# Query weight restacked in the first batch, and each later key matrix from 16 matmuls of 128 rows and 16 of 64

## Chip, cores and metric

The kernel runs on one core of one Trainium2 chip. The time is the device time of one execution in microseconds; lower is better.

## The reference

Eight sequences (batches) of 1024 rows and 1024 columns pass through cross-attention with a context of 64 rows each, and then through a linear layer in simulated fp8, both with a residual:

```
x = x + xattn(layernorm(x), ctx, Wq, Wkv, Wout)
    qp = q @ Wq.T ;  k, v = split(ctx @ Wkv.T)          # 16 heads of 64
    scores = (qh . kh) / 8, causal mask over 1024 x 64
    attn = softmax(scores) ;  out = (attn @ vh) @ Wout.T
x = x + ffn(layernorm(x), weight)
    both operands quantised to e4m3 by their largest magnitude,
    out = (x8 @ w8.T) * scales, rounded to bf16
```

## The kernel before

*What it computes with.* Sequences are cut into tiles of 128 rows: TB = 8 tiles in a batch, B = 8 batches, T = 64 tiles. Queries are never formed. For each batch a key matrix M = Wq' K' is made, 1024 columns (16 heads of 64 keys) by 1024 input columns, in CT = 8 pieces of 128 input columns; scores of a tile are then x times M (`scores`, matmuls in L730). In the same way N holds the values times Wout, and the output of a tile is p times N (`split_product`, L746). Numbers are carried as a high and a low half in f16, and a product is three matmuls: high by high, high by low, low by high (`PASSES`, L349). A tile takes 48 matmuls in L730 and 48 in L746.

*How a key matrix is made before.* `make_m(ct, n)` (L675) makes piece ct. For each of the NP = 8 pairs of heads j it goes through the three passes, and in each pass issues two matmuls (L683): the even head on partitions 0 to 63 (`EVEN`) and the odd head on 64 to 127 (`ODD`). Each has 64 rows of contraction, 128 columns of weights and 64 columns moved, so a piece is 48 matmuls. The weights come from `wq_nat[s]` (s = 0 high, 1 low half of Wq; rows of head pair j on the partitions) and the moving side from `k_rows[:, s, j]`, or for batch 0 from `k_split` (`first_m`, which calls `make_m`). The even heads' results go to one PSUM bank, the odd heads' to another (`place`). Pieces alternate between the PSUM regions ps_p and ps_x; a region is free again when ScalarE has taken the high half (L994) and VectorE the low half (L1271) of the piece before it: `grow_full`, `grow_hi`, `grow_free`.

*Where it stands in the order.* The pieces for batch b+1 are made in the seventh tile step (tt = TB - 2 = 6) of batch b, two at a time: pieces 0 and 1 inside the scores of tile t+1 behind chunk 6 (`KEYS_AT_S`), and pieces 2 and 3, 4 and 5, 6 and 7 inside the output product of tile t (`KEYS_AT_O`). The pieces for N are made in a like way with matmuls of 64 rows by 64 columns (L713). That makes 28 such places in the kernel for batches 1 to 7; batch 0's are made before the first tile.

*SP's queue* issues all DMAs in a fixed order: in each step the store of the finished tile (L478), at tt = 0 (for batch 0 at tt = 3) the keys of the next batch from DRAM (`next_k`, `load_k`, L421), at tt = 5 the values, then the load of x four tiles ahead (L403), the DMA transpose of x two tiles ahead (`turn_x`, L429), the second load of x for the residual (L403) and the transpose of p (`turn_p`, L432). In batch 0 the FFN weight (`load_w8`, L471) is loaded in two halves behind steps 2 and 4, to `w8_raw`, which until then holds `k_split`. VectorE first reads it in steps 2 to 5 of batch 1 (`AMAX_AT`).

The stages of a tile on VectorE and ScalarE (layer norm, softmax, splits into halves, residual) run one or two tiles ahead of, or behind, TensorE's. After the last tile the FFN phase runs (L903), from about 1485 us.

Of the kernel before, what the change touches and what calls it, by code (L numbers as in the profile page):

```python
# [25 lines left out]
F16 = mybir.dt.float16  # L26
# [7 lines left out]
P = 128  # L34
# [22 lines left out]
def xattn_ffn_kernel(nc, x, ctx, Wq, Wkv, Wout, Wffn, out):  # L57
# [3 lines left out]
    NP = NH // 2  # L61
# [13 lines left out]
    with ExitStack() as scope:  # L75
# [12 lines left out]
        wo_t = sb("wo_t", [P, 2, NP, H], F16)  # L88
        m_buf = sb("m_buf", [P, 2, CT, H], F16)
        n_buf = sb("n_buf", [P, 2, NP, H], F16)  # L90
        k_rows = sb("k_rows", [P, 2, NP, SK], F16)
        v_rows = sb("v_rows", [P, 2, NP, SK], F16)

        w8_raw = sb("w8_raw", [P, CT, H], BF16)
# [73 lines left out]
        wkv_t = wo_t[:, 1].rearrange("p j c -> p (j c)").bitcast(F32).rearrange("p (a q) -> p a q", a=LT)  # L168
        w8_flat = w8_raw[:].rearrange("p j c -> p (j c)").bitcast(F16)
        k_split = [w8_flat[:, i:i + 4096].rearrange("p (j k) -> p j k", k=KEYS) for i in (0, 4096)]  # L170
        V_SLOTS = (9, 10, 11, 2)
        v_split = [tile_space[:, i, :].bitcast(F16).rearrange("p (s j k) -> p s j k", s=2, k=KEYS) for i in V_SLOTS]
        wq_nat = [wq_stack[:].rearrange("p (j e) c -> p e j c", e=2)[:, s] for s in (0, 1)]
# [31 lines left out]
        kv_stored = sem("kv_stored")  # L205
        got_k = sem("got_k")
        got_v = sem("got_v")
        got_xa = [sem("got_xa0"), sem("got_xa1")]
        got_xr = [sem("got_xr0"), sem("got_xr1")]
        var_ready = sem("var_ready")  # L210
# [182 lines left out]
        def _(sp):  # L393
# [23 lines left out]

            def load_k(of):

                for s in range(2):  # L420
                    sp.dma_start(k_rows[:, s], of(s)).then_inc(got_k, 16)  # L421

            def load_v(of):
                for s in range(2):
# [49 lines left out]
            def step(b, tt, e, t):  # L474
                known = isinstance(t, int)
                if not (known and (t == 0 or t > KEPT)):
                    sp.wait_ge(x1_ready, t + 1)
                    sp.dma_start(x1_dram[bass.ds((t - 1) * P, P), :], x1[1 - e]).then_inc(x1_stored[1 - e], 16)  # L478
                if is_step(tt, 3 if b == 0 else 0) and not (known and t >= T - TB):
                    next_k(b + 1)  # L480
                if is_step(tt, 5) and not (known and t >= T - TB):
                    next_v(b + 1)
                if not known or t + 2 < T:
                    sp.wait_ge(x_lo, t + 3)
                    if not known or t + 4 < T:
                        load_x(xa, got_xa, t + 4, e)
                    turn_x(t + 2, e)
                if not known or t + 1 < T:
                    sp.wait_ge(p_lo, t + 2)
                    load_x(xr, got_xr, t + 1, 1 - e)  # L490
                    if not (known and t + 2 == T):
                        turn_p(t + 1, 1 - e)
                if b == 0 and tt in (2, 4):
                    sp.wait_ge(k_stored, 32)
                    load_w8(tt // 2 - 1)

            for b in range(B):
                batch(sp, b, step, unroll=b in (0, B - 1))
# [99 lines left out]
        def _(pe):  # L598
# [73 lines left out]
            expand(7)  # L672


            def make_m(ct, n, keys=lambda s, j: k_rows[:, s, j, :]):  # L675
                to = grow_ps[ct % 2]
                if not is_step(n, 0):
                    pe.wait_ge(grow_free[ct % 2], n)
                for j in range(NP):
                    for i, (ws, ks) in enumerate(PASSES):  # L680
                        for k, rows in enumerate((EVEN, ODD)):
                            h = 2 * j + k
                            mm = nc.tensor.matmul(to[:, place(h) * SK:(place(h) + 1) * SK],  # L683
                                                  wq_nat[ws][rows, j, ct * P:(ct + 1) * P], keys(ks, j)[rows],
                                                  start=(i == 0), stop=(i == len(PASSES) - 1))
                mm.then_inc(grow_full[ct % 2], 1)

            def first_m(ct):
                make_m(ct, ct // 2, lambda s, j: k_split[s][:, j, 0:SK])


            WOUT_FREE = ((kv_read, 7), (grow_free[0], 4), (grow_free[1], 4), (wout_lo, 1), (wout_lo, 2),
# [79 lines left out]
            def step(b, tt, e, t):  # L772
# [5 lines left out]
                if not known or t + 1 < T:  # L778
# [2 lines left out]
                    pe.wait_ge(x_turned, 16 * t + 32)  # L781
                    pe.wait_ge(s_read, t + 1)
                    if m_next:
                        pe.wait_ge(got_k, 32 * b + 32)
                        if b == 2:
                            pe.wait_ge(w_scale_made, 1)
                        if b >= 3:
# [928 lines left out]
```

## Time and profile before

| | us |
|---|---|
| median of 3 runs | 1732.33 |
| lowest and highest | 1732.08, 1732.6 |
| the profiled execution's own time | 1734.19 |
| its span, first to last instruction | 1732.3 |
| TensorE busy with matmuls, share of the span | 98% |
| TensorE weight loads, share | 47% |
| VectorE busy, share | 77% |
| ScalarE busy, share | 39% |

Engines are PE (TensorE's matmuls), PEld (TensorE's weight loads, which overlap PE), DVE (VectorE), ACT (ScalarE), POOL (GpSimd) and SPq (the queue on which SyncE issues DMAs). A matmul's end is modelled: its record is longer than the time until the next one starts, so the distance from start to start is what it takes in a dense stream. In a timeline a row is a run of like instructions, with its start, its length to the end of the last one, and how many there are.

### The profile page before, as it was taken

The page shows a single profiled execution, that of the slowest core. Times are in us where ns is not written, and L with a number is a line of the kernel's source. Part 1 is how long each engine was busy: PE and PEld are TensorE (multiplying, and loading weights), DVE is VectorE, ACT ScalarE, POOL GpSimd, SP SyncE. Part 2 cuts the span into 40 slices and gives each one's busy share as a digit, 9 for nine tenths or more (in the row PEclk, how much of TensorE's full clock was granted, in tenths as well). Part 3 has the DMA queues.
Part 4 walks back from the last instruction along what each step waited for, and adds up shares of the span by engine and source line. Part 5 has one row for each costly group of instructions (what it writes and reads, how often), then busy time and mean ns, then how long its engine had stood idle before and what let it go on. Part 6 is the DMA issues. An engine that isn't in the chain of part 4 may idle for free.

```text
span 1732.3 us, 27825 instructions
## 1 busy us (share of the span) xinstructions
PE 1705.6 (98%) x11485; PEld 809.8 (47%) x11513; DVE 1336.9 (77%) x1910; ACT 671.8 (39%) x638; POOL 182.7 (11%) x142
## 2 busy tenths in 40 slices
PE   7999999999999999999999999999999999999998
PEld 4544444445444544454445444544454444544444
DVE  7977687788866887788778877787779666877786
ACT  5632243223322332233223322332233222799985
POOL 0000000000000000000000000000000002255565
PEclk9999999999999999999999999999999999999999
DMA  9346645553545555545454445544544443799997
GB/s 351 105 106 168 152 90 126 135 143 93 128 121 131 111 124 114 140 108 128 121 128 123 119 126 130 113 106 126 132 124 110 97 86 74 263 310 331 320 251 216
DMA packets 387977, 258.95 MB, mean 149 GB/s; under 512 B 341920, under 2 KB 344480, under 8 KB 387616
## 3 DMA queue, kind: packets, MB, share of 16 engines
q1 hardware_dynamic: 387872, 257.47, 56.3%
q8 instruction: 76, 1.25, 0.3%
q14 instruction: 29, 0.24, 0.0%
HBM read 113.25 MB, written 67.11 MB: 104 GB/s over the span
## 4 chain that ended last, share of the span: by engine, by line
PE 86%; DVE 10%; ACT 2%; DMA 1%; issue 1%; SPq 0%; DVEq 0%; ACTq 0%
PE ps_all L730 36%; PE ps_all L746 33%; PE ps_all L903 12%; DVE m_buf L1271 3%; PE ps_all L713 3%; PE ps_all L683 1%; PE ps_all L755 1%; DVE tile_space L1340 1%; DVE hsum L1334 1%; DVE tile_space L1282 1%; DVE tile_space L1328 1%; PE ps_all L832 1%; DVE hmax L1323 1%; ACT tile_space L1007 1%; ACT tile_space L1011 1%
## 5 line engine op out<-in xcount | busy, mean ns | idle before, releaser
L730 PE MATMUL ps_all<-m_buf,tile_space 128*128 128x504 f16 x3072 | 667.7, 376 | 0.6 <-DVE m_buf L1271 0.3
L746 PE MATMUL ps_all<-n_buf,tile_space 128*128 128x512 f16 x3024 | 667.4, 379 | 0.5 <-DMA tile_space<-tile_space 0.5
L730 PEld LDWEIGHTS ps_all<-m_buf,tile_space 128*128 128x128 f16 x3072 | 297.8, 98 | 351.8 <-issue 6.7
L746 PEld LDWEIGHTS ps_all<-n_buf,tile_space 128*128 128x128 f16 x3024 | 293.1, 98 | 356.5 <-issue 7.0
L575 POOL TENSOR_TENSOR rstd_x<-veps_x,minus_half 128x1 f32<-128x1 f32 x64 | 35.3, 551 | 1397.1 <-DVE veps_x L1295 1397.1
L1015 ACT ACTIVATE tile_space<-tile_space,neg_mean 128x1024 f32<-128x1024 f32 x56 | 64.4, 1149 | 279.6 <-DVE neg_mean L1360 279.6
L1011 ACT ACTIVATE tile_space<-tile_space,score_scale 128x1024 f32<-128x1024 f32 x64 | 73.4, 1147 | 232.3 <-DVE tile_space L1328 232.3
L1007 ACT ACTIVATE tile_space<-tile_space 128x1024 f16<-128x1024 f32 x64 | 67.6, 1056 | 190.3 <-DVE tile_space L1340 190.3
L1282 DVE SCALAR_TENSOR_TENSOR tile_space<-tile_space 128x1024 f16<-128x1024 f32 x64 | 78.4, 1225 | 70.7 <-ACT tile_space L1007 70.7
L1334 DVE TENSOR_REDUCE hsum<-tile_space 128x16 f32<-128x1024 f32 x64 | 77.9, 1217 | 58.3 <-ACT tile_space L1011 58.3
L1277 DVE SCALAR_TENSOR_TENSOR tile_space<-tile_space 128x1024 f16<-128x1024 f32 x64 | 78.3, 1223 | 52.8 <-ACT tile_space L1001 52.8
L903 PE MATMUL ps_all<-wo_t,wq_stack 128*128 128x512 bf16 x482 | 114.0, 379 | 0.7
L1001 ACT ACTIVATE tile_space<-tile_space 128x1024 f16<-128x1024 f32 x64 | 67.6, 1056 | 113.5 <-DVE tile_space L1300 113.5
L1323 DVE TENSOR_REDUCE hmax<-ps_all 128x16 f32<-128x1008 f32 x64 | 77.1, 1204 | 30.8 <-PE ps_all L730 30.5
L989 ACT ACTIVATE n_buf<-ps_all 128x1024 f16<-128x1024 f32 x64 | 62.7, 1020 | 85.6 <-PE ps_all L713 85.6
L1632 DVE SCALAR_TENSOR_TENSOR n_buf<-ps_all,n_buf 128x1024 f32<-128x1024 f32 x64 | 78.2, 1221 | 22.4 <-ACT n_buf L1161 20.9
L1271 DVE SCALAR_TENSOR_TENSOR m_buf<-ps_all,m_buf 128x1008 f16<-128x1008 f32 x64 | 75.1, 1202 | 24.2 <-ACT m_buf L994 24.2
L1348 DVE SCALAR_TENSOR_TENSOR tile_space<-ps_all,out_scale,tile_space 128x1024 f32<-128x1024 f32 x56 | 71.7, 1280 | 27.0 <-PE ps_all L746 27.0
L903 PE MATMUL ps_all<-wo_t,tile_space 128*128 128x512 bf16 x389 | 89.8, 379 | 1.2 <-ACT tile_space L1168 0.4
L1265 DVE SCALAR_TENSOR_TENSOR n_buf<-ps_all,n_buf 128x1024 f16<-128x1024 f32 x64 | 75.9, 1219 | 13.5 <-ACT n_buf L989 13.5
L1168 ACT ACTIVATE tile_space<-ps_all,small 128x1024 bf16<-128x1024 f32 x63 | 70.2, 1114 | 30.8 <-PE ps_all L903 28.8
L1289 DVE BATCH_NORM_STATS2 stats_a<-tile_space 128x6 f32<-128x512 f32 x128 | 81.7, 680 | 0.0
(170 smaller groups left out, 1565.9 us busy)
## 6 DMA issues: line engine op xcount, KB each, us to landing
tile_space<-in_x_dram SPq DMA_DIRECT2D x128, 512.0 KB, 4.0
x_scratch<-tile_space SPq DMA_DIRECT2D x56, 512.0 KB, 3.1
m_buf<-x_scratch SPq DMA_DIRECT2D x32, 512.0 KB, 5.6
out_dram<-m_buf SPq DMA_DIRECT2D x32, 512.0 KB, 4.3
tile_space<-x_scratch SPq DMA_DIRECT2D x24, 512.0 KB, 6.0
out_dram<-tile_space SPq DMA_DIRECT2D x24, 512.0 KB, 5.1
m_buf<-in_L_xattn_Wq_dram SPq DMA_DIRECT2D x4, 1024.0 KB, 12.0
n_buf<-in_L_xattn_Wout_dram SPq DMA_DIRECT2D x4, 1024.0 KB, 13.1
```

The source lines that it names most:

```text
L730: mm = nc.tensor.matmul(ps_s[:, half * HALF:half * HALF + RH], left[:, ls, c * P:(c + 1) * P], m_buf[:, rs, c, half * RH:(half + 1) * RH], ...
L746: mm = nc.tensor.matmul(to[:, cols], left[:, ls, j * P:(j + 1) * P], right[:, rs, j, cols], start=(c == 0 and i == 0), stop=(c == CT - 1 a ...
L903: mm = nc.tensor.matmul(y_ps[e][:, cols], left[:, c * P:(c + 1) * P], w8_t[:, c, cols], start=(c == 0), stop=(c == CT - 1))
L1007: nc.scalar.activation(p_rows2[:, 0, :], pr, ACT.Copy, scale=P_SCALE).then_inc(p_hi, 1)
L1011: nc.scalar.activation(ex, sub, ACT.Exp, scale=score_scale[:]).then_inc(exp_done, 1)
L1271: nc.vector.scalar_tensor_tensor(out=keys_of(1, c), in0=rest_of(grow_ps[c % 2][:]), scalar=M_SCALE, in1=keys_of(0, c), op0=ALU.mult, op1=A ...
L1277: nc.vector.scalar_tensor_tensor(out=x_rows2[:, 1, :], in0=xn[e], scalar=XN_SCALE, in1=x_rows2[:, 0, :], op0=ALU.mult, op1=ALU.subtract).t ...
L1282: nc.vector.scalar_tensor_tensor(out=p_rows2[:, 1, :], in0=pr, scalar=P_SCALE, in1=p_rows2[:, 0, :], op0=ALU.mult, op1=ALU.subtract).then_ ...
L1289: nc.vector.bn_stats(stats_a[:, half, :], xa[e][:, half * HALF:(half + 1) * HALF]).then_inc(a_stats, 1)
L1323: nc.vector.tensor_reduce(by_bank(hmax[:]), rest_scores, AX.X, ALU.max).then_inc(max_done, 1)
L1334: nc.vector.tensor_reduce(hsum[:], heads(ex), AX.X, ALU.add).then_inc(sum_done, 1)
L1632: nc.vector.scalar_tensor_tensor(out=a_t[e], in0=u_ps[e], scalar=ROUND_LEAST, in1=v_t[e], op0=ALU.max, op1=ALU.add).then_inc(a_done, 1)
```

## The change

The low half of the query weight and the keys are laid out anew. In steps 1 to 3 of batch 0 five DMAs within SBUF swap halves of `wq_nat`, so that `wq_nat[0]` then holds, for each even head, the high half on partitions 0 to 63 and the low half on 64 to 127, and `wq_nat[1]` for each odd head the low half on 0 to 63 and the high half on 64 to 127. `low_moved`, over the memory of `w8_raw`, is the place between. `load_k` loads the high half of the keys twice, on both halves of the partitions: `k_rows[:, 0]` for even heads, `k_rows[:, 1]` for odd heads, and the low half to `k_rows[:, 2]`. So one matmul of 128 rows gives high by high plus low by high for a head. `make_m` then issues for each pair j two matmuls of 128 rows (one a head) and two of 64 rows (high weight by low key): 32 for a piece, with accumulation groups now of two matmuls a head. The first batch's pieces are made as before by `first_m`, which has the old loop. The FFN weight's halves are loaded behind steps 6 and 7 of batch 0, and TensorE waits once for the restacked weight.

```diff
-        k_rows = sb("k_rows", [P, 2, NP, SK], F16)
+        k_rows = sb("k_rows", [P, 3, NP, SK], F16)
+        low_moved = w8_flat.rearrange("p (j c) -> p j c", c=H)
+        w_moved = sem("w_moved")
             def load_k(of):
-                for s in range(2):
-                    sp.dma_start(k_rows[:, s], of(s)).then_inc(got_k, 16)
+                for k, head in enumerate((EVEN, ODD)):
+                    for rows in (EVEN, ODD):
+                        sp.dma_start(k_rows[rows, k], of(0)[head]).then_inc(got_k, 16)
+                sp.dma_start(k_rows[:, 2], of(1)).then_inc(got_k, 16)
+
+            def stack_wq(tt):
+                if tt == 1:
+                    sp.wait_ge(k_stored, 32)
+                    for k in range(2):
+                        sp.wait_ge(grow_full[k], 4)
+                    for to, of in ((ODD, EVEN), (EVEN, ODD)):
+                        sp.dma_start(low_moved[to], wq_nat[1][of]).then_inc(w_moved, 16)
+                if tt == 2:
+                    sp.wait_ge(w_moved, 32)
+                    sp.dma_start(wq_nat[1][ODD], wq_nat[0][ODD]).then_inc(w_moved, 16)
+                if tt == 3:
+                    sp.wait_ge(w_moved, 48)
+                    for k, rows in enumerate((ODD, EVEN)):
+                        sp.dma_start(wq_nat[k][rows], low_moved[rows]).then_inc(w_moved, 16)
...
-                if b == 0 and tt in (2, 4):
-                    sp.wait_ge(k_stored, 32)
-                    load_w8(tt // 2 - 1)
+                if b == 0 and tt in (1, 2, 3):
+                    stack_wq(tt)
+                if b == 0 and tt in (6, 7):
+                    sp.wait_ge(w_moved, 80)
+                    load_w8(tt - 6)
...
-            def make_m(ct, n, keys=lambda s, j: k_rows[:, s, j, :]):
+            def make_m(ct, n):
                 to = grow_ps[ct % 2]
-                if not is_step(n, 0):
+                pe.wait_ge(grow_free[ct % 2], n)
+                head = lambda h: to[:, place(h) * SK:(place(h) + 1) * SK]
+                for j in range(NP):
+                    for k in range(2):
+                        nc.tensor.matmul(head(2 * j + k), wq_nat[k][:, j, ct * P:(ct + 1) * P], k_rows[:, k, j, :],
+                                         start=True, stop=False)
+                    for k, rows in enumerate((EVEN, ODD)):
+                        mm = nc.tensor.matmul(head(2 * j + k), wq_nat[k][rows, j, ct * P:(ct + 1) * P],
+                                              k_rows[rows, 2, j, :], start=False, stop=True)
+                mm.then_inc(grow_full[ct % 2], 1)
+
+            def first_m(ct):
+                n = ct // 2
+                to = grow_ps[ct % 2]
+                if n > 0:
                     pe.wait_ge(grow_free[ct % 2], n)
...
                     if m_next:
-                        pe.wait_ge(got_k, 32 * b + 32)
+                        pe.wait_ge(got_k, 80 * b + 80)
+                        if b == 0:
+                            pe.wait_ge(w_moved, 80)
```

## Rows read from the trace of the kernel before

**Rows 1.** The page: busy time by engine, granted clock in 40 slices, chain, two groups.

```profile
PE 1705.6 (98%) x11485; PEld 809.8 (47%) x11513; DVE 1336.9 (77%) x1910; ACT 671.8 (39%) x638; POOL 182.7 (11%) x142
PEclk9999999999999999999999999999999999999999
PE 86%; DVE 10%; ACT 2%; DMA 1%; issue 1%; SPq 0%; DVEq 0%; ACTq 0%
L730 PE MATMUL ps_all<-m_buf,tile_space 128*128 128x504 f16 x3072 | 667.7, 376 | 0.6 <-DVE m_buf L1271 0.3
L746 PE MATMUL ps_all<-n_buf,tile_space 128*128 128x512 f16 x3024 | 667.4, 379 | 0.5 <-DMA tile_space<-tile_space 0.5
```

**Rows 2.** Waits, 104 to 1467 us, TensorE: in total, times, longest, in us.

```profile
PEld ps_all L713 <- issue: 11.8, 28, 0.4
PEld ps_all L683 <- issue: 8.9, 21, 0.4
PEld ps_all L683 <- DVE m_buf L1271: 4.4, 14, 0.4
PE ps_all L746 <- DMA tile_space<-tile_space: 0.5, 1, 0.5
```

**Rows 3.** Busy time in a stretch: bounds, length, PE, PEld, DVE, ACT, POOL, clock, DMA.

```profile
205.00:245.00 40.00, 39.91 (x541) 20.81 (x540) 30.60 (x47) 14.16 (x15) 1.10 (x2) 1.00 0.47 107
```

**Rows 4.** Timeline of TensorE, parts of batch 0: start, length in us, instructions.

```profile
146.16 10.36 PE L730 MATMUL ps_all<-m_buf,tile_space 128*128 128x504 f16 x48
...
187.28 2.93 PE L730 MATMUL ps_all<-m_buf,tile_space 128*128 128x504 f16 x13
...
197.48 10.52 PE L746 MATMUL ps_all<-n_buf,tile_space 128*128 128x512 f16 x48
207.84 7.81 PE L730 MATMUL ps_all<-m_buf,tile_space 128*128 128x504 f16 x36
215.59 1.57 PE L683 MATMUL ps_all<-k_rows,wq_stack 64*128 64x64 f16 x96
217.09 2.72 PE L730 MATMUL ps_all<-m_buf,tile_space 128*128 128x504 f16 x12
...
233.34 1.83 PE L683 MATMUL ps_all<-k_rows,wq_stack 64*128 64x64 f16 x96
235.10 1.24 PE L730 MATMUL ps_all<-m_buf,tile_space 128*128 128x504 f16 x5
```

**Rows 5.** The key matmuls' line in batches 1 to 7: durations in ns, forms.

```profile
L683 PEld LDWEIGHTS ps_all<-k_rows,wq_stack x2688: 92/95/97, 215.6 to 1298.8; 64*128 64x128 f16 x192
L683 PE MATMUL ps_all<-k_rows,wq_stack x2688: 189/190/201, 215.6 to 1298.9; 64*128 64x64 f16 x192
```

**Rows 6.** Timeline of TensorE in short windows at the first block's edges.

```profile
215.28 0.38 PE L730 MATMUL ps_all<-m_buf,tile_space 128*128 128x504 f16 x1
215.59 0.20 PE L683 MATMUL ps_all<-k_rows,wq_stack 64*128 64x64 f16 x2
...
216.91 0.25 PE L683 MATMUL ps_all<-k_rows,wq_stack 64*128 64x64 f16 x6
217.09 0.60 PE L730 MATMUL ps_all<-m_buf,tile_space 128*128 128x504 f16 x2
```

**Rows 7.** The same where a block of L713 ends, batch 0.

```profile
98.59 0.63 PE L713 MATMUL ps_all<-wo_t,v_rows 64*64 64x512 f16 x8
99.15 0.39 PE L746 MATMUL ps_all<-n_buf,tile_space 128*128 128x512 f16 x1
```

**Rows 8.** Full-height matmuls of 128 columns: timeline, and their line's durations in ns.

```profile
1469.94 0.61 PE L755 MATMUL ps_all<-ident_half,tile_space 128*128 128x128 f16 x8
...
L755 PE MATMUL ps_all<-ident_half,tile_space x16: 216/219/220, 1468.2 to 1470.3; 128*128 128x128 f16 x16
```

**Rows 9.** Timeline of SP's queue in batch 0 and at batch 1's first step.

```profile
125.90 3.31 SPq L432 DMA_TRANSPOSE tile_space<-tile_space  x1
...
135.19 3.51 SPq L429 DMA_TRANSPOSE tile_space<-tile_space  x1
...
148.91 0.58 SPq L471 DMA_DIRECT2D w_raw<-in_L_ffn_weight_dram  x1
...
150.08 3.55 SPq L421 DMA_DIRECT2D k_rows<-kv_scratch  x2
155.38 1.40 SPq L403 DMA_DIRECT2D tile_space<-in_x_dram  x1
...
165.99 3.59 SPq L432 DMA_TRANSPOSE tile_space<-tile_space  x1
...
176.31 3.29 SPq L429 DMA_TRANSPOSE tile_space<-tile_space  x1
...
262.67 1.90 SPq L421 DMA_DIRECT2D k_rows<-kv_scratch  x2
271.30 0.35 SPq L403 DMA_DIRECT2D tile_space<-in_x_dram  x1
```

**Rows 10.** DMA issues of the kernel: count, KB each, median us to landing.

```profile
kv_scratch<-w_raw SPq DMA_DIRECT2D x2, 1024.0 KB, 8.0
...
w_raw<-in_L_ffn_weight_dram SPq DMA_DIRECT2D x2, 1024.0 KB, 6.6
...
tile_space<-tile_space SPq DMA_TRANSPOSE x127, 5.5
...
v_rows<-tile_space SPq DMA_DIRECT2D x8, 32.0 KB, 2.2
```

**Rows 11.** Busy time around the clock's fall and in the FFN phase's start.

```profile
26.00:28.00 2.00, 0.30 (x1) 0.14 (x1) 1.93 (x5) 1.80 (x4) 0.00 (x0) 1.00 1.02 406
28.00:32.00 4.00, 3.96 (x18) 3.63 (x19) 3.48 (x9) 2.17 (x4) 0.00 (x0) 0.57 1.03 410
...
1498.00:1502.00 4.00, 2.37 (x17) 1.05 (x15) 3.79 (x5) 3.65 (x4) 0.20 (x1) 1.00 0.34 66
```

More of the change, by code:

```diff
@@ L683, in make_m @@
                             mm = nc.tensor.matmul(to[:, place(h) * SK:(place(h) + 1) * SK],
-                                                  wq_nat[ws][rows, j, ct * P:(ct + 1) * P], keys(ks, j)[rows],
+                                                  wq_nat[ws][rows, j, ct * P:(ct + 1) * P], k_split[ks][rows, j, 0:SK],
                                                   start=(i == 0), stop=(i == len(PASSES) - 1))
                 mm.then_inc(grow_full[ct % 2], 1)
-            def first_m(ct):
-                make_m(ct, ct // 2, lambda s, j: k_split[s][:, j, 0:SK])
             WOUT_FREE = ((kv_read, 7), (grow_free[0], 4), (grow_free[1], 4), (wout_lo, 1), (wout_lo, 2),
```

## Prediction, made before the changed kernel was run

> **What bounds the kernel now.** I read the page first, then the totals of waits on the middle of the run, then TensorE's timeline of one batch's seventh tile step (tt = 6), and last short windows at the edges of one block of key matmuls. The page gives TensorE 98% of the span at a granted clock of nine tenths or more in every slice, and the chain that ended last lies 86% on TensorE, 36% in L730 (scores) and 33% in L746 (output product) [rows 1]. The waits say the same more sharply: from 104 us to 1467 us TensorE's matmuls wait for another engine or a DMA once, 0.5 us at L746 [rows 2]. VectorE is busy 30.60 of 40 us around the step that the change touches [rows 3]. So in this stretch every nanosecond that the change adds to TensorE's own stream is a nanosecond of the span, and the question is only how long the new stream takes.
>
> **The stream as it is.** In the step that starts at 207.84 us there are four blocks of 96 key matmuls, each block two key matrices of 48 [rows 4]. Seven batches have them: 28 blocks, 2688 matmuls [rows 5]. A dense L730 stream has 48 matmuls in 10.36 us of which the last one's modelled 0.376 us is its tail: 9.98 / 47 = 0.212 us from start to start [rows 4, 1]. The block's edges differ from that [rows 6]:
> - Going in: the last L730 starts at 215.28 and the first key matmul at 215.59, 0.31 us later where 0.212 is usual: 0.096 us more.
> - Inside: the two matmuls of a pair (even and odd head, upper and lower 64 rows) start within 0.01 us of each other, both done 0.20 us after the first began, at 0.19 us each. The last pair starts at 217.16 - 0.19 = 216.97; from 215.59 that is 47 steps in 1.38 us, 0.029 us for a pair, so two matmuls of 64 rows run side by side in the time of one. 64 columns at 2.4 GHz are 0.027 us.
> - Going out: the first full-height L730 starts at 217.09, 0.12 us after the last pair, where 0.029 would follow: 0.092 us more. The L730 after it starts at 217.69 - 0.376 = 217.31, 0.22 us on, about 0.01 above the usual.
>
> The same is seen where L713 (64 rows by 64 columns) ends: the last of eight starts at 99.22 - 0.38 = 98.84, L746 at 99.15, 0.31 against 0.216 [rows 7]. It is no semaphore: no wait is charged at these edges, only "issue", in 28 of 28 entries of L713 and in 21 of L683 [rows 2]; and L730 runs on from L746 through its own waits with no added gap, 197.48 to 207.84 in 48 steps of 0.216 [rows 4]. What the edges share is that the row height changes between 128 and 64. Price of one change of height: 0.092 to 0.096 us.
>
> **The change, part by part.** (1) *Count of matmuls.* Before, a head pair j takes 3 pairs, 3 x 0.029 = 0.088 us. After, it takes 2 full-height matmuls, one after the other, and 1 pair: again 3 time slots, if a full-height matmul of 64 columns takes a slot of 0.029 us. The trace has no such matmul. Its bounds: 0.029 from below (64 columns stream in 0.027), and from above 0.056, the spacing of full-height loads with 128 columns: 8 in 0.61 us, (0.61 - 0.219) / 7 [rows 8]. I take the lower one, since the pairs load two 64 x 128 weights in every 0.029. So 48 matmuls become 32 and nothing is saved: the removed ones ran beside others.
>
> (2) *Order.* In the new loop j runs full, full, pair, and then full again. A key matrix changes height 16 times, where before a block of two changed it twice. Working for one j: full to full 0.029 + 0.01 (the second matmul after a change, as going out) = 0.039; full to pair 0.029 + 0.096 = 0.125; within the pair 0.003; pair to the next full 0.122. Sum 0.289 us. A block has 16 of these, 4.62 us; before it took 217.09 - 215.28 - 0.21 = 1.60 us. That is 3.02 us more in each block, 28 x 3.02 = 84.6 us. Nothing covers it, because TensorE waits for nobody there.
>
> (3) *What is given back.* The fourth block takes 1.76 us instead of 1.50 (233.34 to 235.10 against 215.59 to 217.09): its second matrix waits for VectorE's L1271, 14 times in the kernel with 4.4 us, and two of those waits belong to a batch [rows 4, 2]. With each matrix three times as long, VectorE, which has 1.21 us for a matrix, is done before. That returns 7 x 0.26 = 1.8 us. Behind the later blocks x, p and the residual come later by as much as TensorE does, so no other wait turns up; VectorE and ScalarE only get slack.
>
> (4) *The first batch.* Restacking adds five SBUF to SBUF transfers of 1 MB on SP's queue: two behind the transpose that ends its issue at 129.21, one in the place of the weight load at 148.91, two after 169.58 [rows 9]. SP itself is held for 0.6 us for each, as by that load. They go ahead of the transposes issued at 135.19 and 176.31 (L429), whose product TensorE takes up at 146.16 and 187.28; a transpose lands 5.5 us after issue, leaving 5.5 us of slack at both [rows 4, 9, 10]. A 1 MB move takes 6.6 us (HBM to SBUF) or 8.0 (SBUF to HBM) from issue to landing [rows 10]; a 32 KB move takes 2.2. If the second's 2.2 us overlap the first's data, two take 6.6 + 4.4 = 11.0 us, else up to 16, so from 129.8 they last until between 141 and 146. Behind 141 the transposed x is in by 145, in time; behind 146 it is in at 149, 3 us late, and that twice. Bounds 0 and +6 us; I take 0, because the step of 148.91 already has such a 1 MB and the keys ahead of its transpose with no wait at L730. The waits that SP gains there (stored keys, all first matrices full, the previous move) are met by then, or hold only what is queued behind them: the next x1 store and transposes. The FFN weight comes at steps 6 and 7 instead of 2 and 4; nobody reads it before step 2 of batch 1.
>
> (5) *Keys of a batch.* load_k has 5 transfers of 3072 pieces instead of 2 of 2048. The two hold SP for 3.55 us, or 1.90 later; times 1.5 that is at most 1.8 us more. In batch 0 the next x load waits from 153.63 to 155.38, in batch 1 from 264.57 to 271.30: covered but for 0.1 us, and that inside the 5.5 us above [rows 9]. The keys themselves are used a whole batch later. Cost 0.
>
> Sum: 84.6 - 1.8 = +82.8 us. The profiled execution took 1734.19 us with a span of 1732.3; what lies around the span (1.9 us) does not change, so it would go to 1817.0. The median of the runs shown, 1732.33, is 1.86 lower, and by the same sum it goes to **1815.1 us**.
>
> One rule of the Trainium skill goes beyond the rows here. TensorEngine Tiling (Array Packing), section Key Properties, says that switching the tiling mode, as against the tile, drains the engine. The trace agrees at each block edge (0.092 to 0.096 us), but it shows no switch between two matmuls of 64 columns; by the rule the 840 new switches cost the same there (+82.8), and without it the sum would be about -3.
>
> **Rivals.**
> - *The clock falls.* In the new blocks TensorE streams 24 slots of 0.027 us in 2.31, less than three tenths of the time. The trace has one fall inside the kernel, to 1.2 GHz: after a stretch in which the engine was busy 0.30 of 2.00 us, the mean granted clock from 28 to 32 us is 0.57, which is 3.44 us at half, 1.72 us lost [rows 11]. Against: it stayed at full through 1498 to 1502 with TensorE busy 2.37 of 4.00 us, and the new gaps are 0.1 us each [rows 11]. After every block that is 28 x 1.72 = 48 us, 1863; after half of them 1839.
> - *No drain between short matmuls.* Then a block is 48 slots, 48 x 0.0294 = 1.41, no cost at entry, 0.09 at exit: 1.50 against 1.60. 28 x -0.10 = -2.7 us, **1729.6 us**, the other side (not slower). For it: the height changes are only seen beside 504 and 512 columns on one side. Against: the exit follows a 64-column pair and pays in full. It decides below 7 ns a switch: 840 x 7 = 5.9 us would eat the 2.7 and 0.2% more.
> - *Only one direction costs* inside the loop, say the pair's loads go ahead while the full matmul of the other bank runs: 448 x 0.096 = 43 less, 1772. Against: both directions cost at the edges.
> - *A full-height load is not hidden.* If the second full matmul waits for its load, whose record is 0.095 us long [rows 5], it starts 0.10 after the first instead of 0.039: 448 x 0.06 = 27 more, 1842. Against it: the 0.056 of rows 8. The skill's page TensorE: Matmul & The Clock Gate, section LDWEIGHTS (loading the stationary operand), gives columns / 1.2 ns whatever the rows, 107 ns here, about 1846 us by that estimate; the trace disagrees, it fits such loads in 56 ns.
>
> **How the numbers follow.** Forecast 80%, clock 8%, no drain 5%, one direction 4%, load 3%. The range around the forecast: below, a full slot without the 0.01 (-4.5), a change of height 3 ns cheaper over 896 of them (-2.7) and 2 us for rows read to 10 ns, 1806; above, the full slot at 0.056 (+7.6), 3 ns more (+2.7), transfers (+6), the 1.8 not given back, 1833. The other cases lie outside, 20% together. A measurement of this kernel tells 0.2% (3.5 us) from no change: slower 94%, the same 4% and faster 2%, both from the case without a drain.
>
> **What would show it.** TensorE's timeline: blocks of 64 matmuls, about 4.6 us long, the step at 207.84 about 39 us instead of 27.3; matmuls of the key line at starts 0.04, 0.12, 0.00, 0.12 us apart. "Issue" waits of its loads in hundreds. No wait for a DMA at 146 and 187 us. A granted clock below full in the middle slices, blocks under 2 us, or a first batch longer than 207.84 us at the same place would each make this prediction wrong in its own term.

## The result, and the profile of the changed kernel

The changed kernel takes 1872.26 us (median of 4, 1872.01 to 1875.05) against 1732.3 before: 1.081 times as long, 95% interval 1.0795 to 1.0821, 140 us more. The forecast was slower, by 83 us, with a range that ended at 1833.

The page of the changed kernel first: busy time, granted clock in 40 slices, and the two lines that now make the key matrices (L702 the matmuls of 128 rows, L705 those of 64). Columns as in [rows 1].

```profile
span 1870.0 us, 26089 instructions
PE 1839.8 (98%) x10617; PEld 875.2 (47%) x10617; DVE 1341.7 (72%) x1910; ACT 676.2 (36%) x638; POOL 182.8 (10%) x142
PEclk9999989998999899999999999989998999999999
L702 PE MATMUL ps_all<-k_rows,wq_stack 128*128 128x64 f16 x896 | 106.2, 202 | 0.0
L705 PE MATMUL ps_all<-k_rows,wq_stack 64*128 64x64 f16 x896 | 92.6, 203 | 0.0
```

TensorE still has 98% of the span, with 868 matmuls fewer than before in the records (10617 against 11485; the program issues 896 fewer). New is the line of the clock: five slices of 40 are below nine tenths, where all were full in [rows 1]. Mean granted clock of the span is 0.973, before 0.999.

The timeline of TensorE in short windows at the start of the first block, which answers to [rows 6]:

```profile
222.13 0.38 PE L762 MATMUL ps_all<-m_buf,tile_space 128*128 128x504 f16 x1
222.34 0.22 PE L702 MATMUL ps_all<-k_rows,wq_stack 128*128 128x64 f16 x2
222.49 0.20 PE L705 MATMUL ps_all<-k_rows,wq_stack 64*128 64x64 f16 x2
222.63 0.23 PE L702 MATMUL ps_all<-k_rows,wq_stack 128*128 128x64 f16 x2
222.79 0.20 PE L705 MATMUL ps_all<-k_rows,wq_stack 64*128 64x64 f16 x2
...
226.83 0.23 PE L702 MATMUL ps_all<-k_rows,wq_stack 128*128 128x64 f16 x2
226.99 0.20 PE L705 MATMUL ps_all<-k_rows,wq_stack 64*128 64x64 f16 x2
227.13 4.41 PE L762 MATMUL ps_all<-m_buf,tile_space 128*128 128x504 f16 x12
```

Read the starts. Scores to the first full-height matmul: 0.21, no extra, for no height changes there. From then on a head pair starts every 0.30 us (222.49 to 222.79), where three slots of 0.029 would be 0.09. Finer: full to full 0.04, full to pair 0.125, within the pair 0.004, pair to full 0.131. The block fills 222.34 to 227.13, 4.79 us, where [rows 6] had 215.49 to 217.09, 1.60, counted from the usual 0.21 us behind the last score matmul. The last row has a second thing to see: 12 score matmuls take 4.41 us, which in [rows 4] took 2.72.

Busy time and granted clock in four stretches, columns as in [rows 3]: the block itself, a part of the 12 score matmuls behind it, the second block, and the whole run between launch phase and FFN phase.

```profile
222.34:227.13 4.79, 4.79 (x66) 3.35 (x64) 1.25 (x2) 1.96 (x2) 0.00 (x0) 1.00 0.00 0
227.72:231.13 3.41, 3.41 (x10) 1.21 (x8) 1.71 (x2) 0.53 (x1) 0.00 (x0) 0.50 0.54 153
233.97:238.96 4.99, 4.99 (x65) 3.40 (x64) 2.70 (x3) 2.16 (x2) 0.00 (x0) 0.90 0.00 0
...
104.00:1605.00 1501.00, 1493.83 (x8413) 701.02 (x8412) 1057.00 (x1591) 398.55 (x378) 42.87 (x62) 0.97 0.47 113
```

In the first block the clock is full. Just behind it, it is at 0.50, 1.2 GHz, for 3.41 us of dense scores. The second block ends with the clock already down: it takes 4.99 us at a mean of 0.90. The engine's modelled busy share in the block is 4.79 of 4.79, and it hides that the array streams columns for only 24 slots of 0.027 us in each half of the block.

The third difference is in the first batch. TensorE's waits from 104 to 1605 us, then SP's queue and TensorE's timeline there, and DMA issues with KB and median us to landing:

```profile
PE ps_all L762 <- DMA tile_space<-tile_space: 6.6, 2, 4.0
```

```profile
127.54 1.32 SPq L433 DMA_DIRECT2D w_raw<-wq_stack  x2
...
133.66 10.50 SPq L448 DMA_TRANSPOSE tile_space<-tile_space  x1
...
149.96 7.90 SPq L424 DMA_DIRECT2D k_rows<-kv_scratch  x4
...
170.54 1.31 SPq L440 DMA_DIRECT2D wq_stack<-w_raw  x2
...
177.25 13.10 SPq L448 DMA_TRANSPOSE tile_space<-tile_space  x1
```

```profile
147.11 10.37 PE L762 MATMUL ps_all<-m_buf,tile_space 128*128 128x504 f16 x48 [2.56 <-DMA tile_space<-tile_space]
...
192.43 12.06 PE L762 MATMUL ps_all<-m_buf,tile_space 128*128 128x504 f16 x48 [4.04 <-DMA tile_space<-tile_space]
```

```profile
w_raw<-wq_stack SPq DMA_DIRECT2D x2, 1024.0 KB, 9.6
wq_stack<-w_raw SPq DMA_DIRECT2D x2, 1024.0 KB, 12.0
```

The transposes of x behind each pair of restacking transfers hold SP 10.50 and 13.10 us at issue, where they held it 3.51 and 3.29 in [rows 9], and TensorE's scores wait 2.56 and 4.04 us for them. The 12.06 us of the second scores, against 10.36, are again the clock, after that wait.

Three sources stand side by side: longer blocks, a lower clock, waits of the first batch. The experiments take them apart. Times are medians, each compared with the kernel before on the same chip (1732.6 to 1733.0 us).

### The profile page after: what moved, and what is told of

Read it like the earlier page. It is cut to its first block, busy times and chain, and to the rows that moved or that the text cites. A ratio compares the mean times of both kernels' runs of the same rounds, so it can differ in the third digit from the quotient of the medians.

```text
span 1870.0 us, 26089 instructions
## 1 busy us (share of the span) xinstructions
PE 1839.8 (98%) x10617; PEld 875.2 (47%) x10617; DVE 1341.7 (72%) x1910; ACT 676.2 (36%) x638; POOL 182.8 (10%) x142
## 4 chain that ended last, share of the span: by engine, by line
PE 91%; DVE 5%; DMA 2%; ACT 1%; issue 0%; SPq 0%; DVEq 0%; ACTq 0%
PE ps_all L762 34%; PE ps_all L778 34%; PE ps_all L937 12%; PE ps_all L702 4%; PE ps_all L705 3%; PE ps_all L745 2%; DMA tile_space<-tile_space 2%; PE ps_all L787 1%; PE ps_all L866 1%; DVE wq_stack L1273 0%; DVE small L1267 0%; DVE wo_t L1292 0%; DVE n_buf L1299 0%; DMA tile_space<-_L_xattn_Wkv_expand_dram 0%; DVE tile_space L1279 0%
## 5 line engine op out<-in xcount | busy, mean ns | idle before, releaser
L762 PE MATMUL ps_all<-m_buf,tile_space 128*128 128x504 f16 x3072 | 690.9, 385 | 7.2 <-DMA tile_space<-tile_space 6.6
L778 PE MATMUL ps_all<-n_buf,tile_space 128*128 128x512 f16 x3024 | 685.2, 386 | 0.6 <-DMA tile_space<-tile_space 0.6
L762 PEld LDWEIGHTS ps_all<-m_buf,tile_space 128*128 128x128 f16 x3072 | 303.3, 100 | 376.4 <-issue 40.2
L778 PEld LDWEIGHTS ps_all<-n_buf,tile_space 128*128 128x128 f16 x3024 | 297.3, 99 | 370.4 <-issue 31.0
L1028 ACT ACTIVATE m_buf<-ps_all 128x1008 f16<-128x1008 f32 x64 | 64.6, 1011 | 149.2 <-PE ps_all L705 144.2
L702 PE MATMUL ps_all<-k_rows,wq_stack 128*128 128x64 f16 x896 | 106.2, 202 | 0.0
L705 PE MATMUL ps_all<-k_rows,wq_stack 64*128 64x64 f16 x896 | 92.6, 203 | 0.0
```

What stands on the lines that cost most here:

```text
L702: nc.tensor.matmul(head(2 * j + k), wq_nat[k][:, j, ct * P:(ct + 1) * P], k_rows[:, k, j, :], start=True, stop=False)
L705: mm = nc.tensor.matmul(head(2 * j + k), wq_nat[k][rows, j, ct * P:(ct + 1) * P], k_rows[rows, 2, j, :], start=False, stop=True)
L762: mm = nc.tensor.matmul(ps_s[:, half * HALF:half * HALF + RH], left[:, ls, c * P:(c + 1) * P], m_buf[:, rs, c, half * RH:(half + 1) * RH], ...
L778: mm = nc.tensor.matmul(to[:, cols], left[:, ls, j * P:(j + 1) * P], right[:, rs, j, cols], start=(c == 0 and i == 0), stop=(c == CT - 1 a ...
```

## Experiments

### Is it the change of height? Grouping the matmuls

> The changed kernel, but each key matrix issues its 16 matmuls of 128 rows first and then its 16 of 64 rows, so a block of two matrices changes the row height 4 times instead of 32. Same matmuls, same DMAs. Theory (the change of height costs about 0.13 us of drain each and the long stretch of drains makes the clock fall): a block goes from 4.79 us back to 48 slots x 0.029 + 4 x 0.1 = 1.8 us, no clock falls in the key steps, and what is left is +6 us for the blocks and +8.6 us for the restacking transfers: 1747 us. Rival (a matmul of 128 rows and 64 columns is dear in itself, or the low activity of short matmuls lets the clock fall): the block stays above 3 us and the time above 1800 us.

```diff
-                for j in range(NP):
-                    for k in range(2):
-                        nc.tensor.matmul(head(2 * j + k), wq_nat[k][:, j, ct * P:(ct + 1) * P], k_rows[:, k, j, :],
-                                         start=True, stop=False)
-                    for k, rows in enumerate((EVEN, ODD)):
-                        mm = nc.tensor.matmul(head(2 * j + k), wq_nat[k][rows, j, ct * P:(ct + 1) * P],
-                                              k_rows[rows, 2, j, :], start=False, stop=True)
+                for j0 in range(0, NP, 8):
+                    for j in range(j0, j0 + 8):
+                        for k in range(2):
+                            nc.tensor.matmul(head(2 * j + k), wq_nat[k][:, j, ct * P:(ct + 1) * P], k_rows[:, k, j, :],
+                                             start=(j == 0), stop=False)
+                    for j in range(j0, j0 + 8):
+                        for k, rows in enumerate((EVEN, ODD)):
+                            mm = nc.tensor.matmul(head(2 * j + k), wq_nat[k][rows, j, ct * P:(ct + 1) * P],
+                                                  k_rows[rows, 2, j, :], start=False, stop=(j == NP - 1))
```

Measured: 1744.05 us, ratio 1.007 (1.0053 to 1.0086). TensorE's timeline at the first block:

```profile
219.73 0.63 PE L703 MATMUL ps_all<-k_rows,wq_stack 128*128 128x64 f16 x16
220.29 0.41 PE L707 MATMUL ps_all<-k_rows,wq_stack 64*128 64x64 f16 x16
220.63 0.64 PE L703 MATMUL ps_all<-k_rows,wq_stack 128*128 128x64 f16 x16
221.21 0.41 PE L707 MATMUL ps_all<-k_rows,wq_stack 64*128 64x64 f16 x16
221.55 2.30 PE L764 MATMUL ps_all<-m_buf,tile_space 128*128 128x504 f16 x10
```

The same 64 matmuls now take 1.82 us (219.73 to 221.55) instead of 4.79, with only their order changed. Sixteen full-height ones take 219.73 to 220.29 with the way out, 0.56 us: 15 x 0.029 + 0.125. The clock is full in every block (mean of the span 1.000). The total is 3 us under the expected 1747. That fells the first half of the rival: a matmul of 128 rows and 64 columns is not dear, its slot is 0.029 us.

> The changed kernel, but the product with the low keys is also made with matmuls of 128 rows (the low keys loaded on both halves of the partitions too, 8 key transfers of 64 rows; the product low by low comes in addition): 32 matmuls of 128 rows and 64 columns for a matrix, in the interleaved order of the changed kernel, and no change of row height at all. Theory (only the change of height drains): a block is 64 slots of 0.029 = 1.87 us, no clock falls, 28 x 0.27 = +7.5 us, transfers +8.5, the wait of the fourth block gone -1.8: 1747 us. Rival (the gaps come from switching between PSUM banks or from going back to an open accumulation group, which this order keeps): blocks of 3 to 5 us, over 1790 us.

```diff
-        k_rows = sb("k_rows", [P, 3, NP, SK], F16)
+        k_rows = sb("k_rows", [P, 4, NP, SK], F16)
...
+                for j in range(NP):
+                    for s in range(2):
+                        for k in range(2):
+                            mm = nc.tensor.matmul(head(2 * j + k), wq_nat[k][:, j, ct * P:(ct + 1) * P],
+                                                  k_rows[:, 2 * s + k, j, :], start=s == 0, stop=s == 1)
```

Measured: 1745.12 us, 1.0075 (1.0059 to 1.009). The block:

```profile
219.67 2.03 PE L703 MATMUL ps_all<-k_rows,wq_stack 128*128 128x64 f16 x64
221.53 2.71 PE L760 MATMUL ps_all<-m_buf,tile_space 128*128 128x504 f16 x12
```

64 slots in 1.86 us, one each 0.029, although this order goes back and forth between the banks and reopens each head's sum like the changed kernel. Between the same accumulation pattern at 1.86 and 4.79 us stands nothing but the row height of the second product. That fells the rivals of the banks and of the open sums. One thing no run separates: whether at a change of height the array has to empty, as the word drain says here, or the weights of the other height cannot be loaded ahead. In the changed kernel's trace the weight load behind each change starts only with its matmul (222.489 and 222.493 us, 222.623 and 222.628), and inside a run of one height it starts 0.03 us ahead.

> The changed kernel, but with four matmuls of 128 rows for two head pairs, then the four of 64 rows: 16 changes of height in a block instead of 32. Theory: two head pairs take 0.39 us (0.040 + 2 x 0.029 + 0.125 + 0.004 + 0.029 + 0.004 + 0.131), a block 3.1 us, +43 us for the kernel at full clock, +8.6 for the transfers, -1.8: 1782 us if the clock stays. Rival (the clock falls as often as with 32 changes): 40 us more, 1820 us.

The edit is that of the grouped kernel with 2 in place of 8: `for j0 in range(0, NP, 2)` and twice `range(j0, j0 + 2)`. Measured: 1777.74 us (two runs, 1776.85 and 1778.62), ratio 1.0257 (1.0237 to 1.0278). A block takes 3.09 us, as 16 changes of height should, and the clock is 0.999. The total is 4 us under the 1782: the block was put at 3.13 us, 1 us too much over 28 of them, and the waits for transposes were 4.4 us in its profile, not 6.6, with no fall of the clock behind them. 1733 + 28 x 3.09 - 46.7 (the 28 blocks before, by their starts in the trace) + 5 is 1778.

### Is the rest the clock? The same drains, in shorter stretches

> The changed kernel with its key matrices placed one at a time, each behind another chunk of 6 matmuls of 512 columns, so no stretch of drains is longer than 2.4 us instead of 4.8. As many changes of height as in the changed kernel. Theory (drains cost 87 us at full clock, the rest of the 140 us is the granted clock that falls on a long sparse stretch): mean granted clock back to about 1.00, time 1732 + 87 + 9 = 1828 us. Rival (the falls depend on the share of drains in a step of 30 us, not on how long one stretch is): granted clock 0.973 again and 1872 us.

```diff
-        KEYS_AT_S = {6: (0, 1)}
-        KEYS_AT_O = {2: (2, 3), 5: (4, 5), 8: (6, 7)}
+        KEYS_AT_S = {4: (0,), 7: (1,)}
+        KEYS_AT_O = {1: (2,), 2: (3,), 4: (4,), 5: (5,), 7: (6,), 8: (7,)}
```

Measured: 1829.85 us, 1.0562 (1.0544 to 1.058). The views of cores of this kernel and of the changed one:

```profile
core 0: 1826.7 us, clock 0.997
```

```profile
core 0: 1870.0 us, clock 0.973
```

And the stretch from 200 to 1450 us, first of this kernel, then of the changed one; the eighth column is the granted clock:

```profile
200.00:1450.00 1250.00, 1250.00 (x7476) 598.78 (x7475) 916.80 (x1368) 352.73 (x336) 28.66 (x52) 1.00 0.46 114
```

```profile
200.00:1450.00 1250.00, 1250.00 (x7211) 590.53 (x7212) 883.01 (x1316) 337.36 (x320) 27.55 (x50) 0.96 0.45 111
```

Each matrix takes 2.39 us, 56 of them 134 us, exactly as many drains as in the changed kernel (28 x 4.79 = 134). Split up by six matmuls of 504 or 512 columns, they no longer bring the clock down, and 42 us are gone. Both kernels' TensorE is busy 1250 of 1250 us by the records, so busy share is no guide to this. The only fall of this kernel between 104 and 1800 us is at 148.3, behind a wait for a transpose.

> The changed kernel with each full-height matmul of the key matrices issued three times (the first two results are overwritten by the third): six full-height matmuls and one pair for each head pair instead of two and one pair. As many changes of height, longer blocks: 0.040 + 4 x 0.029 + 0.125 + 0.004 + 0.131 = 0.416 us a head pair, 6.66 us a block. Theory (the clock falls because the array streams so little of the time in a long stretch, and the filler brings that from 0.27 to 0.45): no falls in the key steps, granted clock about 1.00, 1732.8 + 28 x 6.66 - 46.7 + 8.5 = 1881 us. Rival (the drains themselves, or the length of the stretch, bring the clock down, whatever streams between them): clock 0.97, 40 to 60 us more, 1920 us or above.

```diff
-                    for k in range(2):
+                    for n in range(6):
+                        k = n % 2
                         nc.tensor.matmul(head(2 * j + k), wq_nat[k][:, j, ct * P:(ct + 1) * P], k_rows[:, k, j, :],
-                                         start=True, stop=False)
+                                         start=True, stop=(n < 4))
```

Measured: 1881.5 us, 1.0854 (1.0837 to 1.087). The view of cores, and the block's first rows:

```profile
core 0: 1879.9 us, clock 0.998
```

```profile
223.49 0.34 PE L703 MATMUL ps_all<-k_rows,wq_stack 128*128 128x64 f16 x6
223.76 0.20 PE L706 MATMUL ps_all<-k_rows,wq_stack 64*128 64x64 f16 x2
223.90 0.35 PE L703 MATMUL ps_all<-k_rows,wq_stack 128*128 128x64 f16 x6
```

A head pair now takes 0.41 us and a block 6.66, all the drains are there, the stretch is longer, and the clock never falls in a key step. So neither the drains nor the length of the stretch does it alone: the same drains with four more matmuls in each head pair kept the clock. Adding 1792 matmuls that compute nothing new costs 9 us in all. Their own time is 28 x (6.66 - 4.79) = 52 us, which leaves 43 us given back by the clock.

### The first batch's transfers

> The kernel before with the five 1 MB transfers within SBUF alone, at the same places of SP's queue, each writing back what is there already, and with the later load of the FFN weight; the key matmuls and key loads are those of before. Theory (the two pairs of transfers hold up the transposed x in the first batch, 6.6 us of waits, and a clock fall of 1.7 us behind the longer wait): 1741 us, with waits of about 2.6 and 4 us of L730 for a DMA near 146 and 190 us. Rival (those waits come from the key load's five transfers or from the shifted steps): 1732 us.

The transfers write to `low_moved` and back what `wq_nat[1]` had, and the FFN weight is loaded as late as in the changed kernel:

```diff
+                if tt == 1:
...
+                    for to, of in ((ODD, EVEN), (EVEN, ODD)):
+                        sp.dma_start(low_moved[to], wq_nat[1][of]).then_inc(w_moved, 16)
+                if tt == 2:
...
+                    sp.dma_start(wq_nat[1][ODD], low_moved[EVEN]).then_inc(w_moved, 16)
+                if tt == 3:
...
+                    for rows, of in ((ODD, EVEN), (EVEN, ODD)):
+                        sp.dma_start(wq_nat[1][rows], low_moved[of]).then_inc(w_moved, 16)
```

Measured: 1740.86 us, 1.0047 (1.003 to 1.0063), as expected. Its profiled execution was the fastest of four, 1737.92, and has 3.5 us of waits for the transpose, nearly all at the first pair of transfers, and no fall of the clock behind them:

```profile
149.60 10.37 PE L749 MATMUL ps_all<-m_buf,tile_space 128*128 128x504 f16 x48 [3.38 <-DMA tile_space<-tile_space]
...
191.06 10.37 PE L749 MATMUL ps_all<-m_buf,tile_space 128*128 128x504 f16 x48 [0.16 <-DMA tile_space<-tile_space]
```

The transfers alone, then, cost 8 us in the median, with the later weight load. How late the transposes are differs from one profile to the next: the two waits are 2.56 and 4.04 us in the changed kernel, 3.38 and 0.16 here.

> The kernel before with the new key buffer and its five transfers a batch alone: the old pairs of 64 rows read the high keys of even heads from the first third and of odd heads from the second. Half of each high-key load is not used. Theory (3072 pieces instead of 2048 are covered in every batch): 1732.7 us, the same. Rival (they hold up SP's queue in front of the x load and transpose): +1 us for each of 7 batches, 1740 us.

The edit is the new `load_k` with its 5 transfers, and `k_rows[rows, (k, 2)[s], j, :]` in the old L683. Measured: 1732.95 us against 1732.83, 1.0002 (0.9993 to 1.0012). The larger key loads cost nothing.

> The changed kernel with its five restacking transfers one at a step, in steps 1 to 5 of the first batch, instead of two, one and two. Theory (two 1 MB transfers in a row ahead of the transpose of x are what makes TensorE wait 2.6 and 4 us): both waits gone, 1872 - 8.5 = 1864 us, give or take the clock falls that land elsewhere. Rival (a single transfer ahead of the transpose delays it as well): waits of 1 to 2 us in more steps, 1870 us or more.

```diff
-                if b == 0 and tt in (1, 2, 3):
+                if b == 0 and tt in (1, 2, 3, 4, 5):
                     stack_wq(tt)
```

with one transfer in each of the steps. Measured: 1870.93 us, 1.080 (1.0783 to 1.0816); the expected 1864 was missed. TensorE's waits from 104 to 1450 us:

```profile
PE ps_all L764 <- DMA wq_stack<-w_raw: 11.7, 1, 11.7
```

The two waits for transposes are gone, but there is a new one. The last transfer is issued at the end of step 5, at 208.74 us in this trace, and TensorE's wait for the restacked weight stands ahead of the scores of step 6, not ahead of the first key matrix. That was my error in placing it. The next kernel starts at step 0:

> The changed kernel with its five transfers one at a step in steps 0 to 4 of the first batch; in steps 1 to 5 the last one landed behind the start of TensorE's scores at tt = 6, which wait for it. Theory: neither the waits for a transpose near 146 and 190 us nor the one for the restacked weight; the changed kernel less about 8 us, 1864 us. Rival (spacing does not help, each transfer costs about 1.5 us): 1872 us.

Measured: 1864.85 us, 1.0765 (1.0748 to 1.0781), as expected. That is 132.3 us over the kernel before, where the changed kernel is 140.0 over it: the two pairs of transfers cost 7.7 us. Between 104 and 1450 us it has one wait of TensorE for a DMA left, the 0.4 us of L780 that stands in the kernel before too [rows 2]. The clock is 0.974: spreading the transfers does nothing for the blocks.

### Putting it together

> Grouped order and spread transfers together, and the second matrix of each block mirrored: first matrix 16 full-height matmuls then 16 of 64 rows, second matrix 16 of 64 rows then 16 full-height. Two changes of height in a block, as in the kernel before. Theory (the restacked form has as many time slots as the old one, 48 in a block): block 1.61 us, as 1.60 before, the wait of the fourth block (1.8 us in all) gone: 1731 us, no difference that can be measured. Rival (the moved transfers and larger key loads still cost): 1735 us or more.

```diff
+                pairs_first = ct % 2 == 1
+                for part in ((1, 0) if pairs_first else (0, 1)):
+                    first = part == (1 if pairs_first else 0)
+                    for j in range(NP):
+                        for k, rows in enumerate((EVEN, ODD)):
...
+                                                      start=(first and j == 0),
+                                                      stop=(not first and j == NP - 1))
```

Measured: 1746.72 us, 1.008 (1.0067 to 1.0094); the expected 1731 was missed. It shares the transfers in steps 1 to 5 and so the misplaced wait of 11.3 us. Behind the wait the clock stays at half for another 3.2 us, so the two make up 12.9 of the 13.9 us lost. The blocks take what the theory said:

```profile
233.38 0.63 PE L708 MATMUL ps_all<-k_rows,wq_stack 128*128 128x64 f16 x16
233.95 0.64 PE L712 MATMUL ps_all<-k_rows,wq_stack 64*128 64x64 f16 x32
234.52 0.64 PE L708 MATMUL ps_all<-k_rows,wq_stack 128*128 128x64 f16 x16
235.00 1.24 PE L786 MATMUL ps_all<-n_buf,tile_space 128*128 128x512 f16 x5
```

The block starts at 233.38 and the next output matmul at 235.00: 1.61 us before rounding, with two changes of height, as in [rows 6]. The wait in the fourth block did not go, against what was expected: 1.87 us there, and 1.86 before when counted in the same way. A matrix is as quick as it was, and VectorE is no sooner done.

> The mirrored order (two changes of height a block) with the transfers in steps 0 to 4. The blocks took 1.61 us and the fourth 1.87 in the mirrored kernel, as in the kernel before, and its whole loss was one wait of 11.4 us for the last transfer. Theory: 1733 us, no difference to the kernel before. Rival (transfers still cost): 1736 us or more.

Measured: 1732.73 us against 1732.56, ratio 0.9999 (0.999 to 1.0008). With the order mirrored and the transfers in steps 0 to 4 the restacked weight neither costs nor gains. No version of it beats the kernel before, since both forms have 48 slots and two changes of height in a block.

## Why the prediction was wrong

The direction, the mechanism and its first term were right. The sum against what the runs showed:

| term | predicted us | measured us | shown by |
|---|---|---|---|
| blocks at full clock | +84.6 - 1.8 | 28 x 4.79 - 46.7 = +87.4 | trace; singly placed 56 x 2.39 |
| first batch's transfers | 0 (bound +6) | +7.7 | steps 0 to 4 against steps 1 to 3; transfers alone +7.9 |
| granted clock | 0 (rival, 8%) | +44 | its 23 falls in the trace; singly placed 42, filled 43 |
| key loads | 0 | 0 | key loads alone |

Together they give 139, and 140.0 was measured. The 44 is read from the trace alone. Around the key blocks the clock is at half for 99.0 us, in 23 falls. Of these, 80.2 us lie outside the blocks and cost half, 40.1. The 18.8 us inside them make the blocks only 4.1 us longer, since there the starts move to at most 0.174 us apart.

*The clock* is the step that failed. It stood among the rivals at 8% and outside the range, with two reasons against it. One was that a stretch with TensorE busy 2.37 of 4.00 us had kept the full clock [rows 11]. But busy time in the records takes in each matmul's modelled tail, and the changed kernel shows what that is worth: 4.79 of 4.79 us busy, and the clock falls. The other was that each new gap is only 0.1 us. The runs show that many short gaps in a row do what one long wait does: in a block of the changed kernel, at full clock, no matmul starts more than 0.134 us after the one before, and the clock falls behind it; with the same gaps in stretches half as long, or with more matmuls between them, it does not. I had worked out how thin the stream is, 24 slots of 0.027 us in 2.31, and then argued it away with rows that measure another thing. Which property of the stream the clock answers to stays open. The rival's price was near: it put full cost after every block at 48 us, against 44. Some blocks were spared, and some falls lasted longer (six of them 6.83 us) or reached into a block.

The Trainium skill's page TensorE: Matmul & The Clock Gate, section Why this matters for your kernels, advises against idle gaps between bursts of matmuls. The traces agree in part. A fall follows the 4.04 us wait at 192 us, and falls stand at waits of 3.83 and 2.32 us in the filled kernel and of 2.68 us in the one with all matmuls full height. None follows the 3.38 us with the transfers alone, or the 2.85 us of the grouped kernel. And the advice is not enough: around the 28 blocks of the changed kernel the clock fell 23 times with no such gap near.

*The transfers.* The bounds were +0 and +6 and I took 0, because a single 1 MB and the key load had gone ahead of a transpose with no wait at 148.91 us. Two in a row are another case. The transposes landed 13.3 and 15.1 us after their issue, at 146.97 and 192.35, not 5.5. The estimate for the late case, 3 us each time, was close to the waits that came, 2.56 and 4.04 us. It left out the fall of the clock behind the longer wait, 1.7 us, so even the upper bound was too low.

*The drain.* A head pair was 0.289 us and measured 0.300. Nearly all of the error is in one term: pair to full is 0.131, not the 0.122 read at the block's exit in [rows 6], where the pair followed other pairs. Behind a run of pairs it is 0.122 in the grouped kernel too. Full to pair at 0.125 and full to full at 0.04 were right within 0.001. Over 448 head pairs the whole error is 4.6 us. The change of height costs the same between 64-column matmuls on both sides, as the sum assumed; the rival without drains and the one with drains one way have fallen. The Trainium skill's page TensorEngine Tiling (Array Packing), section Key Properties, says that a switch of tiling mode drains the engine, and as far as the cost goes the traces agree: 0.125 and 0.131 us from start to start where 0.029 is usual.

*The slot* of a full-height matmul of 64 columns, the unknown of part (1), is 0.029 us, the lower bound, with a new 128 x 128 weight for each (64 in 1.86 us). The rival of a load that is not hidden has fallen. The Trainium skill's page TensorE: Matmul & The Clock Gate, section LDWEIGHTS (loading the stationary operand), puts a load at columns / 1.2 ns. As the distance between such loads the traces do not bear that out, 29 ns against 107; the record of one load is near it, 98 ns in the median.

*The wait given back* was right for the changed kernel: its fourth blocks take 4.79 us like the others where the clock is full. That the key loads cost nothing was right too (1732.95 against 1732.83 us). The later FFN weight and SP's new waits cost nothing that can be measured, since the kernel with both, the transfers in steps 0 to 4 and the mirrored order is at 1732.73 us against 1732.56.

*The signs.* The starts 0.04, 0.13, 0.00 and 0.13 us apart came as listed. A clock below full and a first batch longer than 207.84 us (here 214.69) were named as signs against the prediction, and both came. The "issue" waits of the loads in hundreds did not: the loads stand idle for 0.04 to 0.05 us at each change of height, and the profile charges no wait to the key lines for that.

## What to carry to other kernels

Count TensorE's work in time slots and changes of tile height, not in matmuls: two matmuls of 64 rows on different halves of the array were one slot, so joining them into one of 128 rows saved nothing, while each switch between the heights cost 0.1 us. If both heights are needed, issue all of one, then all of the other, and let neighbours meet at the same height; sixteen switches a matrix instead of one cost 87 us in drains alone. And where a change makes TensorE's stream thin for some microseconds, give a fall of the granted clock behind it a chance and a price, and do not take the busy share of the records as a sign against it: it stood at 100% where the clock fell.

## What the runs showed of the hardware that was not expected

- The clock falls though the engine never stands still for more than about 0.1 us. Behind the block that ends at 227.13 us it is 0.50 for 3.41 us. Three variants kept it up: as many drains in pieces of 2.39 us, half as many in blocks of 3.09 us, and as many with four more matmuls to a head pair in blocks of 6.66 us. What they have in common was not sought further.
- Extra matmuls that are overwritten were nearly free where they kept the clock up: 52 us of added work, 9 us of added time.
- A DMA transpose issued behind two 1 MB transfers within SBUF holds SP's queue itself for 10.50 and 13.10 us, instead of 3.3 to 3.5, so what is queued behind it is late as well. Behind a single one, in the kernel with the transfers in steps 0 to 4, it holds the queue for 5.39 to 6.02 us at three of the steps, and TensorE does not wait. In pairs the 1 MB transfers took 9.6 and 12.0 us to land (median of each pair), longer than the 6.6 and 8.0 us of moves from or to HBM [rows 10]; issued singly, 7.8 and 8.7.
- Leaving a pair of 64-row matmuls costs 0.131 us when a full-height matmul preceded the pair, and 0.122 after a run of pairs.
